# Attention scores computed per 64-token chunk on two halves of the TensorE columns, in a one-core AdaLN transformer block

## The reference, cut to what matters

```
NH = 16; D = 128; C = 64
qn = _l2norm(q / scale)
kn = _l2norm(k / scale)
gv = beta[..., None] * v
qc, kc, gvc = (to_chunks(qn), to_chunks(kn), to_chunks(gv))
attn = jnp.einsum('bnhid,bnhjd->bnhij', qc, kc)
decay = jnp.exp(-0.1 * dist)
causal = pos[None, :] <= pos[:, None]
mask = jnp.where(causal, decay, 0.0)
out = jnp.einsum('bnhij,bnhjd->bnhid', attn * mask, gvc)
```

## Time and profile before

| | |
|---|---|
| median of 3 runs | 2207.19 us (2204.98 to 2207.63) |
| the profiled execution | 2207.08 us |
| its span in the trace | 2205.3 us |
| granted TensorE clock, mean | 0.997 of full speed |
| busy: PE, PEld | 98%, 83% |
| busy: DVE, ACT, POOL | 53%, 47%, 24% |
| attention part, with L838 | about 50 us to 1362 us |
| expert part | 1362 us to the end |

### The profile page before, as it was taken

One profiled execution on the slowest core, in us unless ns is written; L12 is line 12 of the kernel. 1 busy time (PEld: TensorE's weight loads), 2 busy tenths in 40 slices (PEclk: granted clock), 3 DMA queues, 4 the chain that ended last, 5 costly groups with the idle time before them and its releaser, 6 DMA issues.

```text
span 2205.3 us, 34017 instructions
## 1 busy us (share of the span) xinstructions
PE 2168.8 (98%) x11420; PEld 1839.8 (83%) x11420; DVE 1176.3 (53%) x2171; ACT 1029.9 (47%) x3284; POOL 537.3 (24%) x540
## 2 busy tenths in 40 slices
PE   7999999999999999999999999999999999999999
PEld 6888888888888888888888887888888888888887
DVE  4455566555556555555555454555555555545554
ACT  4555555555555655556555453333333333333332
POOL 2333334344334334434434442000000000000000
PEclk8999999999999999999999999999999999999999
DMA  7464451453553543542333130343334233323221
GB/s 234 168 195 160 163 163 46 153 154 92 154 144 84 172 152 92 147 147 87 127 118 98 53 134 1 139 173 110 120 106 157 97 120 133 120 101 114 92 101 63
DMA packets 191884, 274.66 MB, mean 125 GB/s; under 512 B 99184, under 2 KB 132960, under 8 KB 191712
## 3 DMA queue, kind: packets, MB, share of 16 engines
q1 hardware_dynamic: 191712, 272.49, 38.8%
HBM read 214.79 MB, written 57.67 MB: 124 GB/s over the span
## 4 chain that ended last, share of the span: by engine, by line
PE 91%; DVE 3%; ACT 2%; issue 2%; DMA 1%; SPq 0%; DVEq 0%; ACTq 0%
PE proj_ps L641 47%; PE out_ps L641 14%; PE av_ps L849 5%; PE s_ps L838 4%; PE s_ps L894 3%; PE av_ps L894 3%; PE kt_ps L894 3%; PE qt_ps L894 3%; PE qt_ps L822 2%; PE kt_ps L827 2%; DMA head_scr<-stage 1%; PE misc_ps L669 1%; ACT squares L1062 1%; PE misc_ps L660 0%; PE out_ps L707 0%
## 5 line engine op out<-in xcount | busy, mean ns | idle before, releaser
L641 PE MATMUL proj_ps<-w_qkv,h_t 128*128 128x512 f32 x2304 | 612.3, 404 | 15.1 <-DVE q_sb L1353 6.8
L641 PEld LDWEIGHTS proj_ps<-w_qkv,h_t 128*128 128x128 f32 x2304 | 409.9, 189 | 97.2 <-issue 14.3
L641 PE MATMUL proj_ps<-h_t,w_qkv 128*128 128x512 f32 x1800 | 443.7, 391 | 0.0
L641 PEld LDWEIGHTS proj_ps<-h_t,w_qkv 128*128 128x128 f32 x1800 | 335.9, 188 | 68.9
L598 POOL TENSOR_TENSOR inv_norm<-guarded,minus_half 128x8 f32<-128x8 f32 x128 | 209.6, 1638 | 662.6 <-DVE guarded L1366 662.5
L1053 ACT ACTIVATE q_t<-qt_ps 128x512 f32<-128x512 f32 x128 | 76.3, 596 | 320.6 <-PE qt_ps L822 320.5
L641 PE MATMUL proj_ps<-h_t,w_gate 128*128 128x512 f32 x768 | 186.9, 398 | 0.5 <-PE misc_ps L695 0.3
L1353 DVE TENSOR_TENSOR q_sb<-proj_ps,bias 128x512 f32<-128x512 f32 x128 | 88.0, 687 | 181.0 <-PE proj_ps L641 174.2
L1062 ACT ACTIVATE squares<-q_sb 128x128 f32<-128x128 f32 x512 | 151.5, 298 | 69.2 <-DVE q_sb L1353 65.3
L641 PEld LDWEIGHTS proj_ps<-h_t,w_gate 128*128 128x128 f32 x768 | 142.7, 190 | 32.4 <-ACT gate L1076 2.5
L1353 DVE TENSOR_TENSOR v_sb<-proj_ps,bias 128x512 f32<-128x512 f32 x128 | 88.5, 691 | 138.7 <-PE av_ps L849 138.2
(11 more groups left out here) (202 smaller groups left out, 3292.6 us busy)
## 6 DMA issues: line engine op xcount, KB each, us to landing
w_qkv<-tile_scr SPq DMA_DIRECT2D x100, 768.0 KB, 4.3
w_qkv<-head_scr SPq DMA_DIRECT2D x45, 1024.0 KB, 11.4
head_scr<-stage SPq DMA_DIRECT2D x30, 512.0 KB, 3.1
w_gate<-head_scr SPq DMA_DIRECT2D x15, 1024.0 KB, 4.9
w_out<-head_scr SPq DMA_DIRECT2D x15, 1024.0 KB, 5.3
tile_scr<-stage SPq DMA_DIRECT2D x25, 512.0 KB, 3.2
x_in<-_attn_hidden_states_dram SPq DMA_DIRECT2D x16, 512.0 KB, 7.3
h_scr<-stage SPq DMA_DIRECT2D x16, 512.0 KB, 3.3
```

Source lines behind the costliest of these rows:

```text
L641: mm = pe.matmul(out, w, y, start=(j == 0 and m == 0), stop=(3 * j + m == n - 1))
```

## The change

Each head's score matmul becomes two, one per chunk of 64 tokens. For chunk c the stationary operand is the chunk's 64 keys, the moving operand its 64 queries, and the result goes to partitions 64c to 64c + 63 and to the columns of the same chunk's queries. In the built program the new matmuls carry a tile of 128 rows by 64 columns of the array, at column 0 for the first chunk and at column 64 for the second; all others at L838 and around it carry the whole 128 by 128. The two blocks that pair one chunk with the other are not written any more; they hold what was in the bank before, and the mask still multiplies them by zero. The mask, the semaphores and all else stay.

```
--- before.py
+++ after.py
@@ -833,9 +833,12 @@
                 after(pe, masked, n - 1)
                 if n == 1:
                     pe.wait_ge(gained, 3)
+
+
                 for h in range(HG):
-                    at = slice(h * P, (h + 1) * P)
-                    mm = pe.matmul(s_ps[:, at], k_t[:, at], q_t[:, at], start=True, stop=True)
+                    for c in range(P // CH):
+                        at = slice(h * P + c * CH, h * P + (c + 1) * CH)
+                        mm = pe.matmul(s_ps[c * CH:(c + 1) * CH, at], k_t[:, at], q_t[:, at], start=True, stop=True)
                 mm.then_inc(scored, 1)
```

## The result

| | before | after |
|---|---|---|
| median of 5 runs | 2206.67 us (2204.92 to 2207.63) | 2195.18 us (2193.39 to 2198.72) |
| ratio, 95% interval | 1 | 0.9952 (0.9937 to 0.9966) |
| profiled execution, its span | 2207.08, 2205.3 us | 2196.34, 2194.6 us |

The changed kernel is faster by 0.5%, 11.5 us, where 23.7 were forecast. The sign and the overlap of the two halves were right; the size was not, and 2195 us is within the range stated only because that was wide. It is also, by accident, the time that the prediction gave for d = 30 ns, and we will see that this is not what happened: two terms were wrong in opposite directions.

A forecast was written before the change was run, and what follows sets the result against it. TensorE, busy 98% of the span, was taken to bound the kernel, and weight loads the score block. 110 blocks x -215 ns = -23.7 us, so 2207.1 - 23.7 = 2183.4 us; range 2165 to 2232.

The forecast's parts named there:

- d: Score block: distance at which TensorE can open the next instruction at a change of halves; taken as 15 ns, bounds 0 and 30.
- What bounds the kernel, and what bounds the block: TensorE, busy 98% of the span, bounds the kernel; weight loads, 112 ns per 128 columns, bound the score block.
- (a): Score block: eight pairs of load and matmul become 16; a 64-column load taken as 58 ns, bounds 52 and 64.
- (b): Behind the score block: V's first load, 128 columns, lies beside a 55 ns matmul; its 112 ns count in full.
- (c): Score block if the halves take turns: 982 ns, 86 more than before; about 2217 us, chance 0.34.
- (d): Score block if the halves overlap: 681 ns, 215 less than before; chance 0.48.
- 3 x 146 + 131: Score block with overlapping halves: forecast span between first and last end, about 0.57 us, at 146 ns a head.
- the case priced at -378: Score block if each half ran its eight loads wholly for itself: 518 ns, 378 less; 2165.5 us.
- (e): What reaches the end: 110 of 128 blocks counted, since in 16 + 2 `attend` already waits for the mask; -23.7 us.
- (f): TensorE's queue: 1024 more loads and 1024 more matmuls, their issue hidden as long as it is below 58 ns a pair.
- (g): Mask, semaphores and other engines: the same instructions, at nothing; the mask still 0.69 us over 512 columns.
- 896 - 215 = 681: Score block from first score stream to V's first stream: 896 ns before, 681 forecast with overlapping halves.

The follow-up runs named there:

- e2_same_half: The changed kernel with both chunks' score matmuls on the first half of the columns, the second chunk's scores missing from the result: 2246.22 us.
- e3_chunk_outer: The changed kernel with the chunk loop outside the head loop, eight pairs in a row on one half, then eight on the other: 2222.68 us.
- e5_quarters: The changed kernel with each head's scores in four pieces of 32 keys on the four 32-column groups, 32 pairs a step: 2195.08 us.

## Why the prediction was off, step by step

- **What bounds the kernel, and what bounds the block** (weight loads): right. e2_same_half has the 58.3 ns, and quarters with 32-column loads moved the bound to the moving columns.
- **(a) The half-width load at 58 ns:** right; its record is 138 ns, where 130 to 135 were forecast.
- **(b) V's load behind the block** stands in full: right, but with something ahead of it.
- **(c) or (d), turns or overlap:** overlap, as forecast. What was mis-sized is **d**. I took 15 ns from the middle of 0 and 30, with the halves opening strictly in the written order. The block was 415 ns from first to last end, against 3 x 146 + 131 = 569: each half ran for itself, the case priced at -378, because the other half's instructions pass those that wait (e3_chunk_outer). That is 154 ns more gain a block than the sum had.
- **(e) 110 of 128 places:** too few. The waits of `attend` for the mask did not grow (8.1 us in 18 places before, 7.6 in 17 after), so the waits swallowed nothing of the gain (the spans could not tell 128 x 81 from 110 x 81 ns, 10.4 from 8.9 us). A likely reason, not shown: where VectorE is late it is late by TensorE's own earlier work, and that moved with the rest. The mask hid the earlier scores as worked out.
- **(f), (g):** right; 1024 more pairs cost nothing by their number, and e5_quarters, with 2048 more on top, cost nothing either.
- **The sum:** 896 - 215 = 681 was forecast for the block. With the halves by themselves it would be 518, with the two drains 518 + 287 = 805; measured 896 - 81 = 815. At d = 30 the old sum had 786, which looks close and has nothing to do with it.

## What to carry to other kernels

Cutting a narrow matmul into column tiles shortens only what lies between two changes of the array's division, and only until the moving columns become the bound (quarters of the scores gained nothing over halves); each pair of changes costs about 0.29 us here. So count the blocks first, put as much tiled work as possible into each, and start with the blocks that are bound by their loads and long (the router's 1.7 us) rather than with the short ones. Write the tiles in turn, not one tile's work first. And before a row is used to clear a suspicion, make sure that the instruction in it really is of the kind in question; an instruction's listing is not what the engine is told.

## What the runs showed of the hardware that was not expected

- A change between the whole array and a column tile, in either direction: the first load of the new division opens 71 to 72 ns before the last record of the old one ends (medians). It was so with 16, 32 and 64 columns, behind last records of 183 to 388 ns, and with one tile or all in use. For the score block in halves this makes, as an estimate, 145 ns in and 142 ns out. The 145 has the first load's own 55 ns in it, which nothing hides any more; the way in is 27 ns shorter where that load has 32 columns (173 against 200 ns for the scores, 133 against 160 for the router). On the way out the first projection matmul ends 427 to 430 ns behind the last record in every one of these kernels.
- Two halves: 16 pairs in 415 ns (first to last end); the second eight cost 6 ns. Four quarters: 32 pairs in 411 ns. With 16 moving columns and 32-column loads, 64 pairs in 534 ns, 4.2 ns an instruction.
- About three pairs of one tile can be waiting while the next tile's go ahead, loads and matmuls alike (e3_chunk_outer).
- A plain fp32 matmul of 16 stationary columns leaves the undivided array; an fp32 transpose of 16 columns does not.
